# Routed rows beside the 512-row units in 35 pieces of 128, two to a unit, in place of 21 units of 256

## The reference, cut to what matters

```python
xn = _layernorm(x)
s = attention(xn)                                   # r, k, v, scan, Wo
flat = xn.reshape(-1, 128)                          # 8192 tokens
probs = softmax(flat @ gate_W.T)
top_v, top_i = top_k(probs, 2)
gates = zeros.at[arange(T)[:, None], top_i].set(top_v)
g = silu(einsum('td,edf->etf', flat, w1_e))
u = einsum('td,edf->etf', flat, w3_e)
routed = einsum('te,etd->td', gates, einsum('etf,efd->etd', g * u, w2_e))
shared = einsum('nbsf,nfd->bsd', silu(x w1_s) * (x w3_s), w2_s) / 8
out = x + s * silu(0.5 * shared + 0.5 * routed)
```

## Time and profile before

| | us |
|---|---|
| median of 3 runs | 722.42 (719.79 to 723.98) |
| span of the profiled execution | 719.3 |
| busy: TensorE matmul | 654.1 (91%), 8536 matmuls |
| busy: TensorE weight load | 452.1 (63%) |
| busy: VectorE | 555.4 (77%) |
| busy: ACT | 494.9 (69%) |
| busy: POOL | 478.9 (67%) |

### The profile page before, as it was taken

The page is one execution under the profiler, slowest core; times in us unless marked ns, Lnnn a source line. Parts: engine busy times, 40 slices in busy tenths (PEclk is TensorE's granted clock), DMA queues, the critical chain, the costliest instruction groups (busy, mean ns, idle before and its releaser), DMA issues.

```text
span 719.3 us, 22370 instructions
## 1 busy us (share of the span) xinstructions
PE 654.1 (91%) x8536; PEld 452.1 (63%) x8536; DVE 555.4 (77%) x1058; ACT 494.9 (69%) x1008; POOL 478.9 (67%) x519
## 2 busy tenths in 40 slices
PE   2787897978999999999999999999997899999993
PEld 1544565646665665566666666878886676777772
DVE  5989986877667886667766676667664899999996
ACT  4864798857665656666666666666665788888872
POOL 4844321244777777777777777767778487888873
PEclk9999999999999999999999999999999999999997
DMA  9931111111111323433323334333362767777762
GB/s 243 299 95 45 45 61 46 45 51 36 48 49 49 108 91 108 137 108 108 110 92 109 106 106 139 110 101 108 97 103 93 237 179 230 216 229 222 233 176 59
DMA packets 88616, 86.75 MB, mean 121 GB/s; under 512 B 11394, under 2 KB 65284, under 8 KB 88516
## 3 DMA queue, kind: packets, MB, share of 16 engines
q1 hardware_dynamic: 79428, 66.70, 29.8%
q0 software_dynamic: 9088, 18.63, 9.6%
HBM read 50.82 MB, written 34.47 MB: 119 GB/s over the span
## 4 chain that ended last, share of the span: by engine, by line
PE 53%; DVE 13%; ACT 12%; POOL 11%; issue 7%; DMA 3%; SPq 0%; POOLq 0%; DVEq 0%; ACTq 0%
PE banks L1556 7%; PE banks L1558 7%; PE banks L1557 7%; PE banks L1596 5%; DVE hidden L1218 4%; POOL expert_rows L644 4%; PE banks L1576 4%; PE banks L1577 4%; PE banks L1575 4%; POOL srows L634 3%; ACT hidden L785 3%; PE banks L1621 3%; PE banks L1693 3%; PE banks L1672 3%; ACT rows L823 2%
## 5 line engine op out<-in xcount | busy, mean ns | idle before, releaser
L785 ACT CAST hidden<-hidden 128x512 f16<-128x512 f32 x206 | 127.1, 617 | 135.5 <-DVE hidden L1218 135.4
L634 POOL DMA_INDIRECT srows<-normed_rows,source x142 | 149.7, 1054 | 60.4 <-issue 40.2
L1222 DVE TENSOR_TENSOR hidden<-hidden 128x512 f16<-128x512 f32 x180 | 124.4, 691 | 83.9 <-ACT hidden L785 83.0
L1218 DVE TENSOR_TENSOR hidden<-hidden,banks 128x512 f32<-128x512 f32 x206 | 140.8, 684 | 44.0 <-ACT hidden L781 38.2
L1575 PE MATMUL banks<-wwords,hidden 128*128 (+1 forms) x824 | 148.8, 219 | 1.5 <-DVE hidden L1222 1.1
L1576 PE MATMUL banks<-wwords,hidden 128*128 (+1 forms) x824 | 148.6, 219 | 0.0
L1577 PE MATMUL banks<-wwords,hidden 128*128 (+1 forms) x824 | 148.6, 219 | 0.0
L781 ACT ACTIVATE hidden<-banks 128x512 f32<-128x512 f32 x206 | 122.7, 596 | 28.1 <-PE banks L1558 27.8
L1556 PE MATMUL banks<-sx,wwords 128*128 128x512 f16 (+1 forms) x368 | 121.5, 330 | 3.2 <-DVE wwords L1013 2.7
L1558 PE MATMUL banks<-sx,wwords 128*128 128x512 f16 (+1 forms) x368 | 121.6, 330 | 0.0
L1557 PE MATMUL banks<-sx,wwords 128*128 128x512 f16 (+1 forms) x368 | 121.5, 330 | 0.0
(11 more groups left out here) (218 smaller groups left out, 1429.7 us busy)
## 6 DMA issues: line engine op xcount, KB each, us to landing
rows<-x SPq DMA_DIRECT2D x32, 256.0 KB, 4.9
rows<-expert_rows SPq DMA_DIRECT2D x32, 256.0 KB, 3.6
normed_rows<-rows SPq DMA_DIRECT2D x16, 256.0 KB, 3.9
r_rows<-rows SPq DMA_DIRECT2D x16, 256.0 KB, 2.1
rd_rows<-rows SPq DMA_DIRECT2D x16, 256.0 KB, 2.2
stage<-r_rows SPq DMA_DIRECT2D x16, 256.0 KB, 4.0
k_rows<-rows SPq DMA_DIRECT2D x16, 256.0 KB, 2.2
kd_rows<-rows SPq DMA_DIRECT2D x16, 256.0 KB, 2.2
```

The costliest lines, as they stand in the source:

```text
L634: G.indirect_dma_start(srows[:, q % NXB, t, :], None, rows_in, bass.IndirectOffsetOnAxis(source[:, at:at + 1], 0)).then_inc(sem[f"s_in{q % ...
L785: A.copy(guh[:, i % 4, :], gu[:, i % 2, :]).then_inc(sem["gu_hi"], 1)
L1218: V.tensor_tensor(gu[:, i % 2, :], sg[:, i % 2, :], psum[2 * (i % 2) + 1][:, :], ALU.mult).then_inc(sem["gated"], 1)
L1222: V.tensor_tensor(gul[:, i % 4, :], gu[:, i % 2, :], guh[:, i % 4, :], ALU.subtract).then_inc(sem["gu_lo"], 1)
```

## The change

What remains beside the wide units lies in `HALVES` = 35 pieces of 128 rows, each with an expert of its own. Two pieces share a unit of 256 rows (18 units, the last one half empty), which is fetched, turned, split and stored like before. A narrow unit still has two steps, but a step is now one piece of 128 rows with the whole width of its expert: four pieces of the width for 128 rows in place of two for 256, so that the hidden tile stays 128 x 512. The last unit has one step. There are 59 units in place of 62, 136 half blocks in place of 142, and 199 steps in place of 206. The register with the expert is read for each piece (`half_of`). `PART_STEP` is 68 in place of 75.

```diff
-    ROUTED = 2 * NTOK // UNIT + EXPERTS - 1
     WIDES = (2 * NTOK - EXPERTS * (WIDE - 1) + WIDE - 1) // WIDE
-    NARROWS = ROUTED - 2 * WIDES
+    HALVES = (2 * NTOK - WIDE * WIDES + EXPERTS * (P - 1)) // P
+    NARROWS = (HALVES + 1) // 2
+    ROUTED = 2 * WIDES + NARROWS
...
-    FULLS, RESTS = NTOK // WIDE, (2 * NTOK - WIDE * WIDES) // UNIT
+    FULLS, RESTS = NTOK // WIDE, (2 * NTOK - WIDE * WIDES + P - 1) // P
...
-        steps = [(v, j) for v in range(NU) for j in range(2 if order[v][0] == "narrow" else 4)]
+        steps = [(v, j) for v in range(NU)
+                 for j in range(min(2, HALVES - 2 * order[v][1]) if order[v][0] == "narrow" else 4)]
...
-        PART_STEP = 75
+        PART_STEP = 68
...
-            def weights(v, part, c):
+            def half_of(i):
+                v, j = steps[i]
+                return (v, 0 if wide(v) else j)
+
+            def weights(i, part, c):
+                v, j = steps[i]
                 at = part * WIDTH + c * P
                 if not routed(v):
                     at += EXPERTS * EW
                     return wh[:, at:at + P], wl[:, at:at + P]
-                d = bass.ds(expert_at[v] + at, P)
+                d = bass.ds(expert_at[half_of(i)] + at, P)
                 return wh[:, d], wl[:, d]
...
-                return [(2 * j + c, c * UNIT, UNIT) for c in range(2)]
+                return [(c, c * P, P) for c in range(FC)]
...
+                    if not wide(v):
+                        mh, ml = [a[:, j * P:(j + 1) * P] for a in (mh, ml)]
...
-                parts = [(c, at, t) for c, at, n in columns(i) for t in range(n // P)]
+                parts = [(c, at, t if wide(v) else j) for c, at, n in columns(i) for t in range(n // P)]
                 for n, (c, at, t) in enumerate(parts):
-                    if t == 0:
-                        a, b = weights(v, 2, c)
+                    if n == 0 or not wide(v):
+                        a, b = weights(i, 2, c)
...
-                    load = steps[i][0] + 1 if i < NS and last_step_of(i) and routed(steps[i][0] + 1) else None
+                    load = i + 1 if i + 1 < NS and routed(steps[i + 1][0]) and half_of(i + 1) != half_of(i) else None
```

More of the change, by code:

```diff
@@ L34, with constants @@
 CONST = {}
-def constants(routed):
+def constants(ntok):
     p = np.arange(P)
@@ L53, in constants @@
         "rank": np.repeat(EXPERTS - np.arange(EXPERTS)[None, :], P, 0),
-        "units": np.repeat(UNIT * np.arange(routed)[None, :], P, 0),
+        "units": np.repeat(P * np.arange(4 * (ntok // WIDE + 1))[None, :], P, 0),
         "ones": np.ones((P, 1)),
         "eps": np.full((P, 1), 1e-5),
-        "count": np.repeat(np.arange(max(P, 2 * routed))[None, :], P, 0),
+        "count": np.repeat(np.arange(2 * P)[None, :], P, 0),
         "token": (p[:, None] + 1 + P * np.arange(16)[None, :])[:, None, :] * np.array([1, -1])[None, :, None],
-        "pad": p[:, None] + 1 + UNIT * (routed - EXPERTS + 1),
+        "pad": p[:, None] + 1 + 2 * ntok,
     }
@@ L206, in build @@
         over = late([P, EXPERTS, max(FULLS, RESTS)])
[L207 to L209 removed]
+        eun = late([P, WIDES + HALVES, EXPERTS - 1])
+        eidf = sb("eidf", [P, WIDES + HALVES])
+        eid = sb("eid", [P, WIDES + HALVES], I32)
         dec = sb("dec", [P, 1])
@@ L1062, in dve_fulls @@
                 V.tensor_tensor(over[:, :, 0:FULLS], rep(count, FULLS),
-                                rep_mid(C("units")[:, 2:2 * FULLS + 2:2], EXPERTS), ALU.is_ge).then_inc(sem["route"], 1)
+                                rep_mid(C("units")[:, 4:4 * FULLS + 4:4], EXPERTS), ALU.is_ge).then_inc(sem["route"], 1)
                 V.wait_ge(sem["route"], ROUTE_CHOSEN + 1)
@@ L1187, in dve_unit_experts @@
             def dve_unit_experts():
-                for to, some in ((wide_to, slice(0, WIDES)), (narrow_to, slice(WIDES, WIDES + NARROWS))):
+                for to, some in ((wide_to, slice(0, WIDES)), (narrow_to, slice(WIDES, WIDES + HALVES))):
                     n = some.stop - some.start
@@ L1516, in weights, with pe_expert @@
                     return wh[:, at:at + P], wl[:, at:at + P]
-                d = bass.ds(expert_at[v] + at, P)
+                d = bass.ds(expert_at[half_of(i)] + at, P)
                 return wh[:, d], wl[:, d]
-            def pe_expert(v):
-                kind, i = order[v]
-                if v == FIRST:
+            def pe_expert(i):
+                v, j = half_of(i)
+                if (v, j) == (FIRST, 0):
                     T.wait_ge(sem["unit_experts"], 1)
-                col = i if kind == "wide" else WIDES + i
-                expert_at[v] = T.value_load(eid[0:1, col:col + 1], min_val=0, max_val=(EXPERTS - 1) * EW)
+                col = index(v) if wide(v) else WIDES + 2 * index(v) + j
+                expert_at[v, j] = T.value_load(eid[0:1, col:col + 1], min_val=0, max_val=(EXPERTS - 1) * EW)
             def columns(i):
@@ L1553, in pe_up @@
                     for c, at, n in columns(i):
-                        a, b = weights(v, part, c)
+                        a, b = weights(i, part, c)
                         o = psum[2 * (i % 2) + part][:, at:at + n]
@@ L1572, in pe_down @@
                     o = psum[4 + v % 2][:, t * P:(t + 1) * P]
-                    s = slice(at + t * P, at + (t + 1) * P)
+                    s = slice(t * P, (t + 1) * P) if wide(v) else slice(at, at + P)
                     last = last_step_of(i) and n == len(parts) - 1
@@ L1780 @@
         "w1s": a["ffn_w1_s"], "w3s": a["ffn_w3_s"], "w2s": a["ffn_w2_s"],
-        "const": constants(2 * nb * SEQ // UNIT + EXPERTS - 1),
+        "const": constants(nb * SEQ),
     }
```

2 lines of the change are left out of this document (1 added, 1 removed).

## The result

| | before | after |
|---|---|---|
| median, same chip (4 runs each) | 721.11 us | 748.70 us (747.50 to 749.63) |
| ratio to before | | 1.0383, 95% interval 1.0354 to 1.0412 |
| span of the profiled execution | 719.3 us | 746.9 us |
| forecast | | 743.8 us (729 to 757), +21.4; measured +27.6 |

The account below looks back on a forecast made before the run. It took TensorE's array as today's limit in the narrow stretch and its sequencer as the limit after: +23.5 +1.5 -3.3 -0.3 = +21.4 us on 722.4 gives 743.8 us, range 729 to 757.

Parts of the forecast that it names:

- Rival 1: Narrow steps: register instructions stay hidden and TensorE's array remains the limit; 707 us, chance 0.07.
- rival 2: Narrow steps: a register instruction's slot shrinks to about 0.09 us, so steps take 2.97 us; about 720 us, chance 0.06.
- rival 3: Upward matmuls of 128 columns: weight loads become the limit, 3.46 us a step; about 740 us, chance 0.03.
- rival 4: Narrow steps: TensorE's clock falls to 1.2 GHz, 4.8 us a step; 775 us, chance 0.04.
- The price of a narrow step: Late narrow step on TensorE's sequencer: 24 register instructions 3.0 us, reading 0.65, waits 0.16, together 3.81 us.
- The parts are free: Eight projection parts from step 164 on: no cost beyond (c) and (d), with 3.81 - 2.09 us of array time free per step.
- (b) to (e): From step 164: steps finishing wide ones 9.2 us, finishing shared ones 8.4 (1.0 more for parts), shared unit 9.4, last step's end 6.8.
- The early narrow steps: Steps 48 to 51: three at 2.81 us for about 2.13, one at 3.81 for 3.46; +2.4 us.
- small terms: Shorter ACT instructions on two-hot operands, partly offset by VectorE's routing comparisons and larger constants: -0.3 us, between -1 and +1.
- The waits for fetched rows: Before step 164: TensorE's 3.6 us of waits absorb early delays; of these 0 to 3.7 us remain, taken as +1.5.
- The end: After the last matmul: the last stored rows land 4.2 us later in place of 7.5; -3.3 us.
- The backlog is gone: POOL's last stores: TensorE at 7.6 us per block is slower than POOL's 5.4, leaving one DMA with its issue.

Follow-up runs that it names:

- the kernel with fixed weights: The changed kernel with all 35 narrow pieces taking expert 0's weights, without register addresses or expert-number readings: 789.41 us against 817.9 before on that chip.
- the version with copies: The changed kernel with VectorE copying w1 and w3 of each late piece to a fixed place two steps ahead: 712.30 us, 0.9871 of before.

## Why the prediction was right, and where its terms were off

**The bound and the mechanism: right.** The array's limit gave way to the sequencer's, as the steps at the empty queue said. Rival 1 (hidden) and rival 2 (half hidden) fell to the slots that start 0.124 us apart; rival 3 to the kernel with fixed weights; rival 4 to the clock, 1.00 in 480 to 530 us and in the rest of the narrow stretch. The forecast of 743.8 us is 4.9 us below the measured 748.70, and the difference 6.2 us too small; the places are below. Its bounds, as given, add up to 735 to 760 us, not 731 to 757, which changes nothing here. And the 16 register instructions of the earlier trace rows belong to two steps: besides the 24 upward matmuls, downward ones and a turned block stand between them, so that matmuls cost the sequencer even less than it says.

**The price of a narrow step: 3.81 forecast, 4.04 measured** (mean of steps 176 to 197, in which both parts are narrow; the prediction counts 24 such, so 5.5 us). It is the largest term of the miss. Three quarters of the register instructions from 480 to 560 us start at most 0.13 us behind the one before, the rest later, up to 0.28 us. And a reading takes 0.72 us from its load to the sequencer's third instruction behind it at the mean of the 26 from step 172 on (0.65 at the median), since the load itself is sometimes 0.6 us. With 0.72 and the 0.16 for waits, (4.04 - 0.88) / 24 leaves 0.132 us a slot. The prediction took both from one place each, where they were near their least.

**The parts are free, as said.** The last one follows step 192; the steps 194 to 197, with none near, are 3.91 to 4.24 us, 4.05 at the mean, and a period of four steps with a part is 16.2 us, which is 4 x 4.05.

**The rest of the stretch: 34.8 forecast ((b) to (e)), 33 measured** (what 24 x 4.04 leaves of 130.0). Together this makes +27.3 for the stretch in place of +23.5.

**The early narrow steps: +2.4 forecast, +3.0 measured** (12.9 us from step 48 to 52 in place of 9.8), the same mis-sizing. Step 48 itself stands 1.7 us later, beyond the small terms (-1 to +1); 0.7 of it are there at the first upward matmul already. It doesn't last: the version with copies has step 48 at 171.06 us, near before's 170.99, and step 164 at 448.52, as late as the change. The waits for fetched rows took back 2.2 us by step 164, close to what was said; net +2.5 there for the forecast's +1.2 (early part and small terms).

**The end: -3.3 forecast, -2.2 measured, by another way.** This is the one step whose mechanism failed. "The backlog is gone" does not hold: as `LAG` is 3, the last downward parts follow one another without upward ones between, and the six DMAs of the last units meet at POOL; the landing is 6.0 us behind the last matmul, not 4.2, and only 1.4 us nearer than before. And "the next stage waits for that landing, so this counts" was wrong in its second half: behind the last matmul stand 170.4 us in the kernel before, 168.2 in the change, 167.6 and 167.05 with the landing moved ahead. Of 6 us only 1.0 to 1.5 count. Why the change's end is 2.2 us shorter with a landing 1.4 us nearer isn't shown.

Sum of the spans, by place: +2.5 at step 164, +27.3 behind it, -2.2 behind the last matmul (170.4 to 168.2): +27.6, and the spans differ by 27.6.

## What to carry to other kernels

An address in a register is not free because its instruction is short or because today nothing waits for it. Take its price where the queue is empty, from start to start (here 0.124 to 0.132 us, and 0.65 to 0.72 for a reading), multiply by its number per step, and compare with the array's time of that step: above it it costs all of it, below it little, but not always nothing, as the addresses behind the reading show in the version with copies. When pieces become half as large, the count of addresses doubles while the columns stay, so put what is addressed by number at a fixed place first (here two copies of 0.45 us on VectorE), and look in the timeline for what holds the array then: an engine that is full need not be it, as POOL shows. A wait at a stage's border is worth what moves the next stage's end, and that is found by moving it, not by its length in the chain.

## What the runs showed that was not expected

- A busy share of 88% from 480 to 530 us goes with steps of 4.04 us where the array needs 2.42: matmuls of 0.22 us that start 0.12 us apart leave no idle time in the profile. The starts tell it.
- Two chips pause TensorE's instruction stream. The same kernel before takes 721 and 722 us where there are no pauses and 818 and 829 us on these two; the pauses are spaced 0.7 us, come in clusters, fall on 128-column and 512-column matmuls alike, and stand in the expert units, from 198 us on; the stage behind them takes 168 to 172 us on these chips and 167 to 170 on the others. A window of the kernel with fixed weights shows the clock falling with them (columns as above):

```profile
280.00:300.00 20.00, 18.23 (x151) 11.02 (x148) 15.02 (x31) 11.63 (x24) 12.00 (x11) 1.00 0.24 82
300.00:315.00 15.00, 9.39 (x56) 4.31 (x54) 5.15 (x10) 4.92 (x10) 8.12 (x9) 0.77 0.36 112
```

  56 matmuls start in 15 us there (125 in the same window of the kernel before on the first chip). What pauses the stream wasn't tested.
- The matmuls between two register instructions, with their weight loads, cost the sequencer nothing that can be seen: the slot is 0.124 us with one of them between and with two.
